# Moving the sums of both score paths to the end of the beat in an attention plus feed-forward kernel on one Trainium2 core

## What is computed

```python
L   = einsum(q, k) * scale;  L_y = einsum(q, k_y) * scale        # k_y is a second key projection
agg = sum(exp(clip(L_y, -15, 15)) * mask) + EPS                  # over the keys, causal mask
w   = softplus(log(|L| + EPS) - log(agg + EPS)) * mask
out = (w / (sum(w) + EPS)) @ v;   x = layernorm(x + out @ w_proj.T)
h   = silu(x @ w1 * s1) * (x @ w2 * s2)
h   = gelu(h @ h1 * t1);  h = gelu(h @ h2 * t2);  x = layernorm(x + h @ w3 * s3)
```

## Time and profile before

| | us |
|---|---|
| median of 3 runs | 1240.26 (1237.6 to 1240.6) |
| the profiled execution | 1239.5 |
| its span, first to last instruction | 1237.8 |
| mean granted TensorE clock | 0.988 of full speed |
| PE, DVE, ACT, POOL busy in the span | 96%, 58%, 53%, 17% |

### The profile page before, as it was taken

How to read it: one execution, slowest core, us unless ns; L and a number is a source line. 1 busy time by engine, 2 the same in 40 slices (tenths; PEclk the granted TensorE clock), 3 DMA queues, 4 the chain that set the end, 5 groups by cost and what they waited for, 6 DMA issues and landing times.

```text
span 1237.8 us, 23984 instructions
## 1 busy us (share of the span) xinstructions
PE 1184.8 (96%) x8222; PEld 805.6 (65%) x8222; DVE 714.9 (58%) x1178; ACT 659.0 (53%) x1004; POOL 205.5 (17%) x238
## 2 busy tenths in 40 slices
PE   6899999999999999879999999999999999999997
PEld 2444444544444444437888888888888888888886
DVE  3577778787878787875345435344344353443444
ACT  4688989899888888755114133232242332322421
POOL 2434333434333333300000000000000000000000
PEclk7999999999999999989999999999999999999999
DMA  5555758576776765277000100001000001000010
GB/s 150 120 141 136 215 158 223 156 228 166 216 191 186 204 169 144 56 234 268 34 34 1 36 16 17 34 0 34 17 0 34 17 17 34 0 34 17 0 34 18
DMA packets 62544, 117.28 MB, mean 95 GB/s; under 512 B 8992, under 2 KB 14624, under 8 KB 62496
## 3 DMA queue, kind: packets, MB, share of 16 engines
q1 hardware_dynamic: 62064, 116.12, 32.9%
q10 hardware_dynamic: 432, 0.52, 0.2%
HBM read 46.35 MB, written 19.92 MB: 54 GB/s over the span
## 4 chain that ended last, share of the span: by engine, by line
PE 80%; DVE 9%; issue 5%; ACT 4%; DMA 1%; DVEq 0%; POOL 0%; ACTq 0%; POOLq 0%; SPq 0%
PE score_banks L1360 53%; PE acc_bank L1272 8%; PE score_banks L1244 6%; DVE w_ring L904 4%; PE misc_bank L1236 3%; PE misc_bank L1199 3%; PE misc_bank L1340 2%; ACT w_ring L656 2%; ACT e_ring L649 1%; PE misc_bank L1303 1%; DVE base_v L957 1%; DVE e_ring L895 1%; PE misc_bank L1207 1%; PE misc_bank L1319 1%; DVE e_ring L889 1%
## 5 line engine op out<-in xcount | busy, mean ns | idle before, releaser
L728 ACT ACTIVATE f_h_full<-score_banks,f_scales 128x512 f32<-128x512 f32 x128 | 87.5, 689 | 340.8 <-PE score_banks L1360 340.7
L904 DVE TENSOR_TENSOR w_ring<-score_banks,keep 128x1024 int32<-128x1024 int32 (+1 forms) x192 | 194.0, 1040 | 28.1 <-PE score_banks L1244 27.3
L1360 PE MATMUL score_banks<-f_ha_hi,f_w_all 128*128 128x512 f32 x512 | 204.0, 399 | 0.0
L1360 PE MATMUL score_banks<-f_hb_hi,f_w_all 128*128 128x512 f32 x512 | 203.6, 398 | 0.0
L1360 PE MATMUL score_banks<-f_hb_lo,f_w_all 128*128 128x512 f32 x512 | 201.6, 394 | 0.0
L1360 PE MATMUL score_banks<-f_ha_lo,f_w_all 128*128 128x512 f32 x512 | 200.8, 392 | 0.0
L656 ACT ACTIVATE w_ring<-w_ring 128x1024 f32<-128x1024 f32 (+1 forms) x192 | 172.5, 918 | 24.3 <-DVE w_ring L904 24.2
L649 ACT ACTIVATE e_ring<-score_banks 128x1024 f32<-128x1024 f32 (+1 forms) x192 | 158.3, 877 | 39.4 <-PE score_banks L1244 36.0
L513 POOL TENSOR_SCALAR_AFFINE_SELECT e_ring<-e_ring 128x512 f32<-128x512 f32 (+1 forms) x96 | 80.4, 837 | 285.8 <-DVE e_ring L895 145.0
L1082 DVE CAST f_ha_hi<-f_h_full 128x512 fp32r<-128x512 f32 x64 | 27.3, 426 | 160.5 <-ACT f_h_full L728 160.5
L1360 PEld LDWEIGHTS score_banks<-f_ha_hi,f_w_all 128*128 128x128 f32 x512 | 96.1, 188 | 24.6
(11 more groups left out here) (143 smaller groups left out, 1759.1 us busy)
## 6 DMA issues: line engine op xcount, KB each, us to landing
piece<-in_wf SPq DMA_DIRECT2D x44, 256.0 KB, 2.9
wf_copy<-piece SPq DMA_DIRECT2D x44, 256.0 KB, 3.0
ky_stack<-ky_hi SPq DMA_DIRECT2D x64, 128.0 KB, 2.4
ky_stack<-ky_lo SPq DMA_DIRECT2D x64, 128.0 KB, 2.4
k_stack<-k_hi SPq DMA_DIRECT2D x64, 128.0 KB, 2.6
k_stack<-k_lo SPq DMA_DIRECT2D x64, 128.0 KB, 2.6
f_w_all<-wf_copy SPq DMA_DIRECT2D x2, 4096.0 KB, 24.6
f_x_turn<-x SPq DMA_DIRECT2D x9, 512.0 KB, 3.2
```

The lines of the kernel that those rows point to most:

```text
L728: nc.scalar.activation(h_full[m % 2][:], f_bank[m % F_RING], ACT.Gelu, scale=scales[:, 1 + layer, m:m + 1]).then_inc(gelu_done, 1)
L904: nc.vector.tensor_tensor(w_ring[:, t % RING, 2 * i:2 * i + 2, 0:cols].bitcast(I32), pair_banks(place(t, i), cols).bitcast(I32), keep[:, a ...
L1360: mm = nc.tensor.matmul(out, left.bitcast(dt), right.bitcast(dt), start=first and n == 0, stop=last and n == 1)
```

## The change

PE's `slot` puts E directly ahead of S at the end of the beat, so the order becomes Y, M, W, M2, E, S. The second `turn` goes behind S at t = 3. The ring of exponentials gets a third buffer. DVE takes the first `absolute` ahead of `clip` at t = 1 and t = 2, and adds up the checks at the start of beat 1 and not at the end. One check moves from t = 4 to t = 5. `beginning` moves two score steps ahead of two projections, and five small matmuls without a use (`STACK_WARM`) are issued while the first stacks are loaded. In `ending` the steps are ordered anew on PE, ACT and DVE, and the last S, the last `project_out` of batch 6 and its `residual` go into the first chunk of the feed-forward layer. The diff, with unchanged lines mostly left out:

```diff
@@ -51,12 +51,14 @@
 RING = 3
-E_RING = 2
+E_RING = 3
 BANK_PAIRS = 3
...
 WARM = 4
-CHECK_BEATS = (0, 2, 3, 4)
+STACK_WARM = 5
+CHECK_BEATS = (0, 2, 3, 5)
 EARLY = (0, CHUNKS)
+FIRST_PAIR = (1, 2)
 CLIPS = (2, 3, 4, 6, 7, 8)
@@ -93,7 +95,7 @@
         at = nc.sbuf_base + -nc.sbuf_base % 32
-        END_ZONE, Y_ZONE, SHARED = 23 * 1024, 80 * 1024, 185 * 1024 - 128
+        END_ZONE, Y_ZONE, SHARED = 23 * 1024, 90 * 1024, 185 * 1024 - 128
 
         def place(zone, start, size):
@@ -762,7 +764,7 @@
                         logs(*beat_before(k, t), 1)
-                    if check_step(t, check) is not None:
+                    if t < 5 and check_step(t, check) is not None:
                         check_piece(k, check_step(t, check))
@@ -774,16 +776,20 @@
                         v_keep(k)
+                    if t == 5 and check_step(t, check) is not None:
+                        check_piece(k, check_step(t, check))
                     if t == 1 and project:
                         ky_keep(k.shift(1))
-                    if t in (2, 3) and output is not None:
-                        turn_keep(output, t - 2)
+                    if t == 2 and output is not None:
+                        turn_keep(output, 0)
                     if t == 4:
...
                         copy_sums(k, 0, (True, 0 in w))
+                    if t == 3 and output is not None:
+                        turn_keep(output, 1)
                     if t == 3 and project and k.half == 1:
@@ -809,25 +815,25 @@
                 keep_att(u, 1, True)
+                base_make(u)
                 logs(k, 0, 1)
+                v_sum_keep(u)
                 logs(k, 1, 0)
-                base_make(u)
                 logs(k, 1, 1)
                 logs(k, 2, 0)
-                v_sum_keep(u)
                 logs(k, 2, 1)
...
                 copy_sums(k, 0, (False, True))
+                logs(k, 3, 1)
+                keep_att(k, 0, False)
+                logs(k, 4, 0)
                 turn_keep(b, 0)
-                logs(k, 3, 1)
-                turn_keep(b, 1)
-                logs(k, 4, 0)
-                keep_att(k, 0, False)
                 logs(k, 4, 1)
                 logs(k, 5, 0)
+                turn_keep(b, 1)
                 logs(k, 5, 1)
+                logs(k2, 0, 0)
                 copy_sums(k, 1, (False, True))
-                logs(k2, 0, 0)
                 logs(k2, 0, 1)
@@ -1074,6 +1080,8 @@
                         lo(c, m - 1, ha_hi, ha_lo)
+                    if done is None and m == 2:
+                        residual(BATCH - 2, 1)
                 lo(c, FT - 1, ha_hi, ha_lo)
@@ -1090,6 +1098,8 @@
             def slot(k, project=True, w=ALL, before=(True, True), next_x=None, divide=None, output=None, norm=None, check=None, **_):
                 for t in range(BEATS):
+                    if t == 1 and check_step(0, check) is not None:
+                        add_differences(k.index - FIRST_CHECK - 1)
                     if t == 1 and before[0]:
@@ -1101,6 +1111,10 @@
                             absolute(k, t, (i,))
+                    elif t in w and t in FIRST_PAIR:
+                        absolute(k, t, (0,))
+                        clip(k, t)
+                        absolute(k, t, (1,))
                     else:
@@ -1128,8 +1142,6 @@
                         add_base(divide)
-                    if t == 1 and check_step(0, check) is not None:
-                        add_differences(k.index - FIRST_CHECK - 1)
 
             def beginning(k, k1):
@@ -1144,24 +1156,23 @@
             def ending(k, k2, b):
                 u = k.shift(-1)
-                absolute(k, 0, (0, 1), w_pair_alone)
+                absolute(k, 0, (0,), w_pair_alone)
                 keep_agg(u, 1)
                 factors(u)
-                absolute(k, 1, (0,), w_pair_alone)
+                absolute(k, 0, (1,), w_pair_alone)
                 qc_make(u)
-                absolute(k, 1, (1,), w_pair_alone)
+                absolute(k, 1, (0, 1), w_pair_alone)
                 absolute(k, 2, (0, 1), w_pair_alone)
+                absolute(k, 3, (0, 1), w_pair_alone)
+                absolute(k, 4, (0, 1), w_pair_alone)
+                sum_differences()
                 divide_sums(b)
-                sum_differences()
-                for t in range(CHUNKS, BEATS):
-                    absolute(k, t, (0, 1), w_pair_alone)
-                absolute(k2, 0, (0, 1), w_pair_alone)
-                residual(b, 0)
-                absolute(k2, 1, (0, 1), w_pair_alone)
-                absolute(k2, 2, (0, 1), w_pair_alone)
+                absolute(k, 5, (0, 1), w_pair_alone)
+                for t in range(CHUNKS):
+                    absolute(k2, t, (0, 1), w_pair_alone)
                 for ct in range(DT):
                     f_turn_lo(0, ct, f_out)
-                residual(b, 1)
+                residual(b, 0)
                 reach(dve, res_made, 2 * b + 1)
@@ -1362,6 +1373,10 @@
             def attention_tail(layer, m):
 
+                if (layer, m) == ("gated", 0):
+                    sum_weights(Unit(BATCH, 1), 2, True)
+                if (layer, m) == ("gated", 1):
+                    project_out(BATCH - 2, 1)
                 if (layer, m) == (0, 1):
@@ -1381,6 +1396,8 @@
                         mm.then_inc(f_ready, 1)
+                    if first:
+                        attention_tail("gated", m)
                 for layer, (name, hi, lo) in enumerate((("h1", ha_hi, ha_lo), ("h2", hb_hi, hb_lo))):
@@ -1457,8 +1474,6 @@
                         v_proj(k)
-                    if sums[0]:
-                        sum_exps(*last, not sums[1])
                     if t in w:
@@ -1467,28 +1482,32 @@
                         ky_proj(k.shift(1))
-                    if t in (2, 3) and output is not None:
-                        turn(output, t - 2)
+                    if t == 2 and output is not None:
+                        turn(output, 0)
                     if t == 2 and norm is not None:
...
                         project_out(output, 0)
+                    if sums[0]:
+                        sum_exps(*last, not sums[1])
                     if sums[1]:
                         sum_weights(*last, not sums[0])
+                    if t == 3 and output is not None:
+                        turn(output, 1)
 
             def beginning(k, k1):
...
                 sum_exps(k, 0, True)
+                scores_y(k, 3, y_pair_alone, 1)
                 ky_proj(k1)
-                scores_y(k, 3, y_pair_alone, 1)
                 sum_exps(k, 1, True)
+                scores_y(k, 4, y_pair_alone, 1)
                 q_proj(k1)
                 sum_exps(k, 2, True)
-                scores_y(k, 4, y_pair_alone, 1)
                 flip_sums(k, 0, (True, False))
@@ -1504,33 +1523,31 @@
                 spread_c(u)
+                sum_values(u)
+                sum_prefixes(u)
                 sum_weights(k, 0, True)
                 scores_w(k, 2, False)
-                sum_values(u)
-                sum_prefixes(u)
                 sum_differences()
+                scores_w(k, 3, False)
                 sum_weights(k, 1, True)
-                scores_w(k, 3, False)
+                scores_w(k, 4, False)
+                sum_weights(k, 2, True)
+                flip_sums(k, 0, (False, True))
+                scores_w(k, 5, False)
+                sum_weights(k, 3, True)
+                scores_w(k2, 0, False)
                 turn(b, 0)
-                sum_weights(k, 2, True)
-                scores_w(k, 4, False)
+                sum_weights(k, 4, True)
+                scores_w(k2, 1, False)
                 turn(b, 1)
-                flip_sums(k, 0, (False, True))
-                sum_weights(k, 3, True)
-                scores_w(k, 5, False)
-                sum_weights(k, 4, True)
-                scores_w(k2, 0, False)
+                sum_weights(k, 5, True)
+                flip_sums(k, 1, (False, True))
+                scores_w(k2, 2, False)
+                sum_weights(k2, 0, True)
                 project_out(b, 0)
-                sum_weights(k, 5, True)
-                scores_w(k2, 1, False)
-                flip_sums(k, 1, (False, True))
-                sum_weights(k2, 0, True)
-                scores_w(k2, 2, False)
                 reach(pe, abs_done, 2 * w_beat(k2, 1) + 2)
                 f_turn_x(0, f_out)
-                project_out(b, 1)
                 sum_weights(k2, 1, True)
-                sum_weights(k2, 2, True)
 
@@ -1543,6 +1560,8 @@
             pe.wait_ge(kind_made[2], 2 * DT)
+            for _ in range(STACK_WARM):
+                nc.tensor.matmul(score[0:2, 2 * BANK_PAIRS - 1, :], ones[:], acc_copy[:], start=True, stop=True)
             pe.wait_ge(kind_in[3], 16)
```

## The result

The changed kernel takes 1260.07 us (median of four runs, 1259.39 to 1265.92) where the kernel before takes 1240.17 beside it. The ratio is 1.0173 with an interval of 1.0155 to 1.019: 19.9 us slower. 1250.0 was forecast, 9.8 slower than the kernel before, so the sign is right and the size is half of what came; the median also lies just above the forecast's own range of 1244 to 1260.

What follows compares the result with a forecast made beforehand. PE was taken to bound attention's middle, busy 317.05 of 328.45 us. Slots +14.5, beginning -2 and ending -2.8 gave +9.7 on 1239.5, so 1250 us; own range 1244 to 1260, 8 in 10 from 1230 to 1261.

Steps and rivals of the forecast that it cites:

- What E and S together save: Slots: adjacent sum steps pay the 0.145 us entry once instead of twice, saving 12.5 us over 86 beats.
- The faster bound, 25 us: Slots: upper bound of the merge's saving, twice the value, if W behind M saves as much again.
- What W now waits for: Slots: without E, W and k_proj wait for ACT; +1.9 per half 1, +0.5 per half 0 slot, +14.5 in all.
- The third buffer and the beginning: Beginning: the third exponentials buffer removes an ACT wait and early Y's feed ACT; -2 us, bounds 0 and -4.
- It is on the path: Beginning: ACT's 1.96 us wait for E delays the whole, because PE waits for these exponentials.
- The early Y(3) and Y(4) feed ACT ahead of the projections: Beginning: two score steps moved ahead of projections give ACT work earlier; part of the -2 us.
- I take this gap away: Ending: DVE's 4.09 us gap vanishes as W precedes S and the turns, -4.1; feed-forward starts 5.3 earlier in all.
- The case of my bound: Ending with moved steps: slower bound of +2 us, if the clock falls again and the gap stays; -2.8 was forecast.
- The steps moved into the feed-forward layer: Feed-forward layer: the steps moved there cost 2.5 us with their entries, as PE has no idle time.
- The wait is covered after all: Rival, slots: W and k_proj wait no longer than now; 1221 us, or about 1232; chance 0.2.
- Ends and slots cancel: Rival: about +5 in the slots and -5 at the ends, no change, 1237 to 1244 us; chance 0.15.
- The clock falls in the slots: Rival: new idle times lower PE's clock once in each of 15 slots, +26 us or 1275; chance 0.05.

Runs made afterwards that it cites:

- experiment 2: Kernel before the change with only E moved directly ahead of S and the third buffer of exponentials: 1259.81 us (1.0165).
- experiment 1: Changed kernel with E put back between M and W in the slots, all else kept: 1244.32 us (1.0034).
- experiment 5: Changed kernel without its five small warm matmuls (`STACK_WARM = 0`): 1261.37 us (1.0193).
- experiment 4: Changed kernel with PE's beginning in the old order, small matmuls and third buffer kept: 1262.57 us (1.0192).
- experiment 3: Changed kernel with the old ending on PE, ACT and DVE, and nothing moved into the feed-forward layer: 1256.73 us (1.013).
- experiment 7: Changed kernel, E behind W only at t = 0 and 3 (after M, M2, W) and at t = 5 without project_out; elsewhere ahead of W: 1245.93 us (1.004).
- experiment 8: Changed kernel with the slots of experiment 7 and the old beginning and ending: 1233.49 us (0.9948).
- experiment 9: As experiment 8, but E and S together only at t = 5 without project_out, M2 behind W again at t = 0 and 3: 1234.15 us (0.9963).
- experiment 10: As experiment 9, but with the mended new ending of experiment 6 in place of the old one: 1232.59 us (0.9956).
- experiment 6: Changed kernel, in its ending each turn_keep one `logs` call later on ACT and the checks' sum two beats earlier on DVE: 1257.12 us (1.0152).
- run 17: A count, not a label: the kernel before, with nothing changed, was run 17 times beside experiments 5 to 8: 1238.0 to 1244.5 us.

## Why the prediction was right, and where it was wrong

**What E and S together save: right.** E and S of 1024 columns were to take 1.86 and take 1.85. Where nothing else changes, at t = 5 of half 1, the beat is 0.14 shorter (4.72 against 4.86), against the fitted 0.145. What PE does in the 0.145 no run shows. The faster bound, 25 us, needed 0.29 a beat and so fell, and the merge is worth some 12.5 in 86 beats by count; no run shows it in the whole kernel by itself. PE's busy time in the loop fell from 317.05 to 311.05, by 6.0; its 60 beats save 8.7 by that count, and where the other 2.7 lie wasn't shown.

**What W now waits for: right, with one beat missed.** W(3) and W(0) start 1.87 and 1.86 behind their Y's, where I had 2.0, so that floor was 0.13 too high. By slot, against the forecast of +1.9 and +0.5: half 1 31.52 to 33.13, +1.6; half 0 34.19 to 34.67, +0.5; an iteration +2.1 against +2.2. Beat by beat in half 1: t = 0 +0.01 (I had +0.13), t = 1 +0.62 (+0.55), t = 2 +0.28 (+0.2), t = 3 +0.16 (+0.29), t = 4 +0.69 (+0.85), t = 5 -0.14 (-0.145). In half 0 t = 4 is +0.94 (+0.85), t = 3 -0.59 (-0.4), t = 2 -0.29 (-0.4), t = 1 +0.13 (+0.4) and t = 0 -0.01 (+0.13). Missed is t = 5 of half 0, +0.30 where I had -0.14: there W is followed by project_out, which waits 0.37 for v_keep on ACT, and E had covered that. The -0.29 of t = 2 came about by luck. I gave it to the `absolute` that now runs ahead of the clip, but experiment 2 hasn't that edit and shows the same 4.40 with no wait ahead of Y(3). There DVE runs without idle time from the clip of t = 1 to the `absolute` of t = 2, as before the change (6.62 us from start to start, 6.36 before), but Y(2) starts 2.99 behind that clip's start in place of 2.41, so this `absolute` starts 3.63 behind its Y in place of 3.95.

Experiments 1 and 2 show that this one edit is the cause of all that the slots lose: without it 15.7 us go, alone it costs 20.2 (1259.81 against 1239.59 beside it). Slot (0,1) is a case apart. It is 0.5 shorter where I had +0.5, since the profile before has 3.41 us at the lower clock there and the one after has none; by the estimate of rows 8 that is worth 1.7, and it is luck.

**The third buffer and the beginning, "I take -2": wrong, +1.8.** Two parts failed. The first is "It is on the path", said of ACT's wait of 1.96. The buffer does away with that wait (in the profile after, six exponentials follow one another with no wait for E), but experiment 2 has the buffer in the old order, and PE's steps there keep their distances apart from 0.4 in a stretch that ran at the lower clock: the wait was beside the path, and the term is worth about nothing. The warm matmuls give 1.0 (experiment 5), within their bounds. The old order with both takes 22.03 (experiment 4), 1.1 less than before, so -1.1 and not -2 was to be had. The second part is what the early Y's do. "The early Y(3) and Y(4) feed ACT ahead of the projections" looked at ACT alone. Y(4) waits 1.42 us for a bank that an exponential must free, and q_proj and E(2), which stand behind it in PE's queue, start at 32.83 and 34.42:

```profile
32.05 0.85 PE L1255 MATMUL score_banks<-q_stack,ky_stack 32*128 32x128 f32 x16 [1.42 <-ACT e_ring L651]
```

ACT then stands idle for 2.31 in its turn until E(2) is done, and its exponentials of Y(4) start at 36.77 us, 17.7 behind the first Y, where it was 15.9 before and 14.8 in experiment 4:

```profile
35.13 0.59 ACT L687 COPY acc_copy<-acc_bank 128x512 f32<-128x512 f32 x1 [2.31 <-PE acc_bank L1283]
...
36.77 2.91 ACT L651 ACTIVATE e_ring<-score_banks 128x1024 f32<-128x1024 f32 x4
```

Experiment 4 gives the 2.9 back in that stretch. For W I had asked in every slot what comes behind it, and I didn't ask it of Y in the beginning. The 1.1 us ahead of the first Y are no step of the change: the first projection starts at 10.16 in this execution against 9.05, on input that came later (DVE's first copy of the weights waits for its DMA until 7.25 us here and until 6.14 before), at 9.1 to 9.4 in experiments 1, 3, 5 and 7 to 9, again at 10.01 in experiment 10, and at 8.9 to 9.0 in the rest. The kernels do the same up to there, so it is taken for a difference between executions.

**The ending, "I take this gap away": the failed step, and the largest miss.** I had the ending 5.3 shorter, and it is 2.7 longer. I followed DVE's backbone and PE's order, and took DVE's 4.09 gap for a matter of PE's queue. It isn't gone but cut up. DVE's timeline has two of the gaps, PE's and ACT's what holds them up (two more, of 2.77 and 3.40, follow on DVE at 574.02 and 578.71):

```profile
564.38 2.36 DVE L910 TENSOR_TENSOR w_ring<-score_banks,keep 128x1024 int32<-128x1024 int32 x2 [1.74 <-PE score_banks L1255]
568.90 2.36 DVE L910 TENSOR_TENSOR w_ring<-score_banks,keep 128x1024 int32<-128x1024 int32 x2 [2.16 <-PE score_banks L1255]
```

```profile
559.39 1.11 PE L1314 MATMUL misc_bank<-ident,acc_copy 128*128 128x128 f32 x4 [2.01 <-DVE ones L988]
...
566.93 1.07 PE L1283 MATMUL acc_bank<-w_ring,v_aug 128*32 128x128 f32 x16 [1.63 <-ACT w_ring L658]
```

```profile
560.82 1.06 ACT L658 ACTIVATE w_ring<-w_ring 128x1024 f32<-128x1024 f32 x1
565.34 0.59 ACT L678 COPY att_t<-misc_bank 128x512 f32<-128x512 f32 x1 [3.46 <-PE misc_bank L1341]
565.82 1.58 ACT L658 ACTIVATE w_ring<-w_ring 128x1024 f32<-128x1024 f32 x2
```

Two waits take the gap's place, and both lie in queues that I hadn't walked. ACT's turn_keep stands ahead of logarithms whose data is ready (the `absolute` ahead of them ended at 562.65) and waits 3.46 us for a turn that PE does late; S waits behind those logarithms (566.93, and 1.21 again at 570.57). PE's flip waits 2.01 for the sum of the checks, which DVE takes up at 559.20, only after the `absolute` of beats 3 and 4 (4.80 from 554.48). Experiment 6 moves only these and the ending takes 33.30. That is 3.0 of the 5.3 that I forecast, with as much of the lower clock as before (6.8), which the forecast of 31 had in it; so 2.3 of the step stay missing even with both queues mended, and no run takes them apart. I had also counted on at most as much of the lower clock as before. A window of such a stretch (the clock is the number behind PE's instructions):

```profile
558.42:565.25 6.83, 5.86 (x32) 0.50 0.99 310
```

In all 13.7 us of the ending are at 0.50, against 6.8 before. The case of my bound came (the clock falls and the gap stays), but I had given it +2 for the ending and the moved steps together, and they measured +4.9 (2.72 and 2.15).

**The steps moved into the feed-forward layer: right,** +2.15 against +2.5, and experiment 3 takes 2.5 away.

**Rivals.** *The wait is covered after all* is refuted by its own mark: it wanted W less than 1.6 behind Y, and W comes at 1.87. *Ends and slots cancel* had the ends at -5; they are +7.7 in all. *The clock falls in the slots* didn't happen in this execution, the loop's clock is 1.00 in spite of waits of 0.24 to 0.79 in most beats. It did happen once each in the loops of experiments 3 and 6, whose slots are those of the full change. A half 1 slot with 3.4 us at the lower clock takes 34.78 there in place of 33.13, near to the 1.7 that the rival counted for each slot (windows of that slot in experiment 6):

```profile
371.73:406.51 34.78, 32.09 (x316) 0.95 0.52 142
```

**Not settled.** Whether the order of the ending has a part in the clock's fall there, and in its length. And whether experiment 10's ending would beat the old one at the same clock: in their profiles the two stretches take 35.86 and 678.30 against 34.53 and 675.74 in 9, the former with 13.7 us at half clock, the latter with 3.4. It wasn't shown. Nor is it known why the first projection comes 1 us late in some executions.

## What to carry to other kernels

An instruction that is moved to be merged with its like may have been the only work between a producer and its consumer: before moving it, look at what starts right after it and how long that has been waiting for something else already. Here 0.14 us per beat were won and up to 0.94 lost. Merge only where other work of that length stays in the gap (here t = 5 with v_proj).

A wait on the engine beside the bound isn't on the path because it is long: take it away and look at what that engine waits for next. Here a wait of 1.96 on ACT went, and PE's steps kept their distances.

When an order is rewritten by hand, walk every engine's queue that it touches, not only the engine that is the backbone. Two entries of ACT's queue and one of DVE's, moved by one or two places, shortened the new ending by 5.7 us (up to some 3 of it by the clock) and made it shorter than the old one.

## What the runs showed of the hardware

Where TensorE's clock falls isn't a property of a stretch of code alone. In the profiles the lower level (0.50) came in pieces of 3.4, 6.8, 10.2, 13.7 and 20.5 us: in the beginning, in slots (0,1) and (7,1), in the ending, and once each in the loops of experiments 3 and 6, while the same loop had none of it in the full change. The endings in the old order had 3.4 to 6.8 us of it (6.8 before and in experiments 3 and 8, 3.4 in 2 and 9). Those in the new order had 6.8 (experiment 6), 10.2 (experiment 5), 13.7 (the full change and experiments 7 and 10), 20.5 (experiment 1) and 24 (experiment 4).

Each kernel was profiled once, and the kernel before, run 17 times beside experiments 5 to 8 with nothing changed, had mean clocks of 0.983 to 0.991 and times of 1238.0 to 1244.5 us. So a difference of a few such pieces between two profiles isn't shown to come from the edit between them. A piece of 3.4 us cost a slot of the loop 1.65, so by estimate 6.8 are worth about 3 us, as large as most of the edits under study: in the profiles of experiments 3 and 4 the slots lost by it what the edited stretch had gained. Edits of that size are to be read from their own stretch, and only then from the median.
